# Layers 0 and 1 of a four-layer convolution kernel: ScalarE's input statistics by a table of their own, and the turn-back one slot later

## The reference

```
# layer 0: the normalised image, shifted down and right by offsets from its own channel means, zero outside
offsets = clip(mean(gn(x), (H, W)) @ W + b, 0, 28).astype(int32)
x = x + where(inside, gn(x)[i - dy, j - dx], 0)
# layer 1: a 3x3 convolution of the signs with the sum of four sign matrices
x = x + conv3x3(sign(gn(x)), sum_m sign(W[m])) + b.sum(0)
# layers 2 and 3: 32 x 32 modes (DCT along columns, real FFT along rows) mixed by R, and a 1x1 convolution
x = x + relu(inverse(R . modes(gn(x))) + gn(x) @ W.T + b)
```

## Time and profile before

| what | us |
|---|---|
| median of 3 runs | 3662.61 (3637.99 to 3672.19) |
| the profiled execution | 3671.81 |
| its span, first to last instruction | 3670.1 |
| mean granted TensorE clock over the span | 0.887 |
| busy in the span: PE, DVE, ACT, POOL | 2996.9, 2730.0, 1511.0, 553.5 |

### The profile page before, as it was taken

How to read it: one execution, slowest core, us unless ns; L and a number is a source line. 1 busy time by engine, 2 the same in 40 slices (tenths; PEclk the granted TensorE clock), 3 DMA queues, 4 the chain that set the end, 5 groups by cost and what they waited for, 6 DMA issues and landing times. The chain is left out here.

```text
span 3670.1 us, 59833 instructions
## 1 busy us (share of the span) xinstructions
PE 2996.9 (82%) x17264; PEld 1392.2 (38%) x17264; DVE 2730.0 (74%) x3908; ACT 1511.0 (41%) x2728; POOL 553.5 (15%) x1059
## 2 busy tenths in 40 slices
PE   0189988888998889889937898888888737999997
PEld 0034443443444334444435333333333316444443
DVE  3888878887888888787233867777776642999998
ACT  3476766766676676674443222222222232000000
POOL 2333323332332333221010000000000010000000
PEclk9988878888888888889867999999999857999998
DMA  5577656666666676664176465655546255999998
GB/s 149 171 221 224 202 183 205 215 202 188 214 198 190 203 219 205 193 199 154 74 147 243 194 260 200 243 220 227 237 201 252 101 121 193 337 373 390 389 378 298
DMA packets 255824, 808.76 MB, mean 220 GB/s; under 512 B 85466, under 2 KB 119774, under 8 KB 244724
## 3 DMA queue, kind: packets, MB, share of 16 engines
q1 hardware_dynamic: 163796, 370.64, 30.8%
q10 hardware_dynamic: 58368, 316.72, 22.2%
q0 software_dynamic: 33376, 118.13, 11.3%
HBM read 479.39 MB, written 329.56 MB: 220 GB/s over the span
## 5 line engine op out<-in xcount | busy, mean ns | idle before, releaser
L975 POOL DMA_DIRECT2D A_rin<-in_x x1008 | 507.5, 504 | 1158.2 <-DVE A_image L818 527.7
L1488 ACT ACTIVATE B_junk<-B_im,B_nk 128x896 bf16<-128x896 f32 x224 | 232.8, 1039 | 717.7 <-DVE B_im L1546 582.9
L476 PE MATMUL A_cps<-A_sign,A_cfull 128*128 128x448 bf16 x1344 | 415.0, 393 | 10.2 <-issue 10.2
L1739 PE MATMUL C_ring<-C_im,C_wnorm 128*128 128x448 f32 x896 | 387.9, 571 | 25.8 <-DVE C_ubuf L1796 20.4
L852 DVE SCALAR_TENSOR_TENSOR A_image<-A_cps,A_cbias,A_image 128x896 f32<-128x896 f32 x224 | 256.9, 1147 | 195.5 <-PE A_cps L476 192.2
L504 PE MATMUL A_aps<-a_k_ident,A_image 128*112 128x128 f32 x1792 | 290.1, 305 | 131.1 <-DVE A_image L852 72.8
L1434 PE MATMUL B_ring<-B_im,B_wnorm 128*128 128x448 f32 x896 | 384.9, 571 | 7.2 <-DVE B_wnorm L1517 5.0
L622 ACT ACTIVATE A_tout<-A_aps 112x512 f32<-112x512 f32 x448 | 249.6, 591 | 333.7 <-PE A_aps L504 214.5
L1406 PE MATMUL B_ring<-B_rout,b_k_rowf 128*64 128x512 f32 x896 | 279.3, 707 | 118.4 <-DVE B_rout L1539 118.4
L481 PE MATMUL A_cps<-A_sign,A_cedge 32*32 32x448 bf16 x1344 | 374.0, 388 | 0.0
L483 PE MATMUL A_cps<-A_sign,A_cedge 32*32 32x448 bf16 x1344 | 373.8, 387 | 0.0
(11 more groups left out here) (198 smaller groups left out, 3697.4 us busy)
## 6 DMA issues: line engine op xcount, KB each, us to landing
A_rin<-in_x POOLq DMA_DIRECT2D x1008, 112.0 KB, 3.7
A_rin<-in_x SPq DMA_DIRECT2D x1008, 112.0 KB, 3.6
x2s<-A_image ACTq DMA_DIRECT2D x112, 896.0 KB, 4.6
B_im<-x2s SPq DMA_DIRECT2D x112, 896.0 KB, 10.2
x3s<-B_im ACTq DMA_DIRECT2D x112, 896.0 KB
C_im<-x3s SPq DMA_DIRECT2D x112, 896.0 KB, 12.9
out<-C_rout ACTq DMA_DIRECT2D x192, 256.0 KB
out<-C_rout ACTq DMA_DIRECT2D x192, 192.0 KB
```

The costliest lines, as they stand in the source:

```text
L476: return nc.tensor.matmul(banks[:, s, 0:LPN], cfull[:, tap, :], lines(n, s, slice(0, P), 0, tap), start=(tap == 0), stop=(tap == 2), skip_ ...
L975: pool.dma_start(rin[slot][32 * i:32 * i + 32, :], rows[:, first * C:(first + CHQ) * C]).then_inc(in_lower[slot], 16)
L1739: nc.tensor.matmul(slot(add_place(e))[:, lane % 2, 0:2 * SIZE], wnorm[par][:], im[par][:, EVN * e:EVN * (e + 1)].rearrange("p (m s) -> p s ...
```

## The change

ScalarE's tiles of input statistics get a table of their own, STAT_BY, one or two in each of slots 1 to 11. X_BY and S_BY are moved: a third input tile in slot 0, the first shifted tile in slot 1. The turn-back of unit n stands in slot n + 2, behind convolution n + 2; with it copy_back, forward_cols (slots 4, 6 to 14, and 15), copy_rows and the ring's numbers. Statistics 0 of VectorE moves from slot 11 to 12, statistics 1 behind the shifted tiles of slot 12, and TensorE's statistics 4 from slot 13 to 14.

```
--- before.py
+++ after.py
@@ -250,8 +250,9 @@
         x_pix = x.rearrange("b r q c -> (b r q) c")
         pad_pix = xpad.rearrange("r q c -> (r q) c")
 
-        X_BY = [2, 4, 6, 7, 8, 10, 11, 12, 14, 16, 16, 16, 16, 16, 16, 16]
-        S_BY = [1, 2, 3, 4, 5, 6, 7, 8, 9, 10, 12, 14, 16, 16, 16, 16]
+        X_BY = [3, 4, 6, 7, 8, 10, 11, 13, 14, 15, 16, 16, 16, 16, 16, 16]
+        S_BY = [0, 1, 2, 3, 4, 5, 6, 7, 8, 10, 12, 14, 16, 16, 16, 16]
+        STAT_BY = [0, 1, 3, 4, 6, 7, 8, 10, 11, 13, 14, 16, 16, 16, 16, 16]
 
         def x_tiles(s):
 
@@ -280,7 +281,7 @@
 
         def stat_tiles(s):
 
-            return x_tiles(s - 1) if s else range(0)
+            return range(STAT_BY[s - 1] if s else 0, STAT_BY[s])
 
         def junk_place(has_v, has_x):
 
@@ -318,7 +319,7 @@
 
             if isinstance(b, int) and b == 0:
                 return 2 * n + half
-            return ((2, 5, 8, 12, 15, 18)[n] if n < 6 else 8 + 2 * n) + half
+            return ((3, 6, 10, 13)[n] if n < 4 else 8 + 2 * n) + half
 
         def spec_step(s):
 
@@ -326,7 +327,7 @@
 
         def ring_t(k):
 
-            return (0, 1, 4, 7, 10, 11, 14, 17)[k]
+            return (0, 1, 2, 5, 8, 9, 12, 15)[k]
 
         def average_no(b, i):
 
@@ -555,22 +556,20 @@
                         conv(b, s)
                     if has_tail and s < 8:
                         spectrum(b - 1, spec_step(s), ring_base(b))
-                    if has_v and s in (3, 5, 7, 9, 11):
-                        forward_cols(b, q, (s - 3) // 2)
-                    if has_v and 1 <= s <= UNITS:
-                        turn_back(b, q, s - 1)
+                    if has_v and s in (4, 6, 8, 10, 12, 14):
+                        forward_cols(b, q, (s - 4) // 2)
+                    if has_v and s >= 2:
+                        turn_back(b, q, s - 2)
                     if has_tail and s == 3:
                         spectrum(b - 1, 4, ring_base(b))
                     if has_x and s in (12, 13):
                         statistics(b + 1, s - 11)
-                    if has_v and s == 13:
-                        forward_cols(b, q, 5)
-                    if has_s and s == 13:
+                    if has_s and s == 14:
                         statistics(b, 4)
+                    if has_x and s == 15:
+                        statistics(b + 1, 3)
                     if has_v and s == 15:
                         forward_cols(b, q, 6)
-                    if has_x and s == 15:
-                        statistics(b + 1, 3)
 
             body(-1, 2, False, True, True, False)
             body(0, 0, True, True, True, False)
@@ -676,8 +675,8 @@
                         copy_rows(b - 1, NSPEC - 1)
                     if has_tail and s < 7:
                         copy_cols(b - 1, spec_step(s), ring_base(b) + ring_t(spec_step(s)))
-                    if has_v and 1 <= s <= UNITS:
-                        copy_back(b, q, s - 1)
+                    if has_v and s >= 2:
+                        copy_back(b, q, s - 2)
                     if has_v and s == 6:
                         copy_rows(b, 0)
                     if has_tail and s == 3:
@@ -692,8 +691,8 @@
                         square(b, q, s - 1)
                     if has_x and s == 14:
                         lower(b + 1, (q + 2) % 3)
-                    if has_v and s in (9, 13):
-                        copy_rows(b, (s - 5) // 4)
+                    if has_v and s in (10, 14):
+                        copy_rows(b, (s - 6) // 4)
                     for k in stat_tiles(s) if has_x else ():
                         x_tile(b + 2, (q + 2) % 3, k, tile_no(b, x_at(k)))
 
@@ -909,8 +908,8 @@
                         add_conv(b, q, s)
                     if has_tail and s == 10:
                         image_statistics(b - 1, far)
-                    if has_x and s in (11, 12):
-                        statistics(b + 1, s - 11, far)
+                    if has_x and s == 12:
+                        statistics(b + 1, 0, far)
                     for k in x_tiles(s) if has_x else ():
                         if k == 0 and has_tail:
                             dve.wait_ge(stored[far], 16 * GROUPS * (third + 1))
@@ -927,6 +926,8 @@
                         signs(q, 2 if s < 5 else 3, (s % 3,) if s < 5 else (s - 6,))
                     for k in s_tiles(s) if has_s else ():
                         add_shifted(b, nxt, k, s_at(k, has_x))
+                    if has_x and s == 12:
+                        statistics(b + 1, 1, far)
                     if has_s and s == 12:
                         center(b)
                     if has_s and s == 13:
```

9 lines of the change are left out of this document (5 added, 4 removed).

## The result

The changed kernel takes 3808.8 us (median of 4 runs, 3789.7 to 3813.7) against 3663.5 of the kernel before: a ratio of 1.039, 95% interval 1.034 to 1.044. That is 145 us slower where 100 were forecast (3763, range 3690 to 3825). The direction and the range held, and so did most of the places. The sum was a third too small, and the experiments show that one of its reasons was wrong.

What follows compares the result with a forecast made beforehand. TensorE was taken to end last from convolution 0 to about 8, then VectorE to the image's end; 4.5 + 0.8 + 1.5 + 0.6 + 0 = 7.4 us an image, times 13.5 = 100 us, giving 3763 us (range 3690 to 3825).

Steps and rivals of the forecast that it cites:

- The wait in front of centered: End of an image: VectorE waits at centered for TensorE's statistics 4, 4.5 us an image, taken between 2.2 and 7.0.
- The idle time itself: TensorE at statistics 1, held by VectorE's later statistics 0: idle up to 5.5 us an image, coming out cold.
- Much slower: Rival: TensorE cold through the turn of the image, centered wait 7.0, 12.2 us an image, 3822 us; chance 0.16.
- The start of the next image: Copy_back 13 behind lower delays forward_cols 6 and convolution 0 by 4.6 us; net 0.8 to add 8 (-1.0 to +1.6).
- What pays it back: By convolution 8 TensorE has one turn-back and one forward_cols less behind it, giving back 3.8 us an image.
- VectorE's extra work behind add 8: End of an image: one shifted tile more and one input tile less on VectorE, 1.5 us (+1.0 to +2.0).
- the 0.6: End of an image: statistics 4's matmul, which ended 0.6 us before centered, now ends right at it, +0.6 us.
- The idle time in front of shifted tiles: Image's front: a third input tile in slot 0 saves at most 37.4 us of load waits over the stage; taken as 0.
- The levelled statistics: ScalarE's regrouped tiles: late copies move from slots 2 and 4 to 3 and 5, two for two, 0 us (-4 to +2).
- the rule: ScalarE's copy is late where a two-tile slot precedes one with a copy and no forward_cols ahead of the turn-back; 1.6 us late.
- Faster: the clock stays up: Rival: copies come in time, gaps and low clock go, net 5 us an image saved, 3598 us; chance 0.12.

Runs made afterwards that it cites:

- e_order: Changed kernel with TensorE's statistics 1 moved behind convolution 13 and turn-back 11, and forward_cols 5 and turn-back 12 ahead of statistics 2: 3753.3 us (1.021).
- e_mean4: Changed kernel with TensorE's statistics 4 directly behind statistics 2, ahead of forward_cols 5 and turn-back 12, and ScalarE's root ahead of copy_back 12: 3821.6 us (1.045).
- e_order_rows: e_order with ScalarE's copy_rows 2 and copy_back 13 also put ahead of root and lower: 3697.2 us (1.011).
- e_parity: Changed kernel with ScalarE's two-tile slots moved from 2 and 4 to 3 and 5, nothing else: 3663.5 us (1.003).
- e_level_odd: e_level with ScalarE's two-tile slots at 3 and 5 in place of 2 and 4: 3761.3 us (1.028).
- e_level: Changed kernel with the turn-back and all that goes with it as before, leaving the levelled statistics alone: 3594.0 us (0.976).
- e_parity_order: e_order_rows with ScalarE's two-tile slots at 3 and 5: 3535.5 us (0.971).
- e_lag: Changed kernel with X_BY, S_BY, ScalarE's statistics tiles and VectorE's statistics 0 and 1 as before, leaving the turn-back's one-slot lag alone: 3680.4 us (1.002).

## Why the prediction was right, and where it was wrong

**The wait in front of centered** (4.5 forecast) was measured at 4.6 to 4.8 us an image, 4.0 to 4.3 in ten images and 6.0 to 6.5 in four: right in place and size, and in its cause, TensorE's idle time at statistics 1 and the chain behind it, in which convolution 13 runs at the lower clock. The idle time itself was mis-sized, 9.4 us where the working had up to 5.5, and was over 5 us in every image. That is the sign that the rival "Much slower" asked for, and still its 7.0 did not come, since the clock was up again by forward_cols 5 in most images. That 4.5 came out so near is in part luck: it was a middle taken between 2.2 and 7.0. As a price, e_order takes the wait away and gains 3.4 us an image by the period (116.6 to 113.1), 4.1 by the medians and 4.8 by the ratios (each over 13.5 images); e_mean4, which takes it away with the same work still between centered and forward_cols 6, gains nothing.

**The start of the next image** (0.8 forecast) is the term that failed. The times were right: forward_cols 6 at 8.3 us, convolution 0 at 11.9. Wrong was the step "What pays it back: by convolution 8 TensorE now has one turn-back and one fc less behind it". It took convolutions 0 to 8 for one path on TensorE. But VectorE waited 5.0 us for convolutions 0 and 1 and then not at all for 2 and 3: there VectorE is the last again, so what it lost at 0 and 1 is lost before any payback. The trace of the kernel before has this too, no wait for a convolution in units 0 to 2 and 0.1 us in unit 3; the prediction read TensorE as last from convolution 0 on. With both waits behind lower out (e_order to e_order_rows) the term measures 5.6 us by the periods, 4.1 by the medians and 2.8 by the ratios; the profiled execution of e_order was its slowest and that of e_order_rows its fastest, so 5.6 is its top. All three are above the 1.6 that the prediction had as the worst. And two things behind lower held forward_cols 6, not one; I read only the copy_back.

**VectorE's extra work behind add 8** (1.5) and the 0.6 were not tested by themselves. The idle time in front of shifted tiles fell by some 3 us an image, which I had put at 0. By size the two would about cancel; no run shows it.

**The levelled statistics** (0, "two for two") was right as a sum and hid the largest effect in the case. The copy waits are 55.9 and 60.2 us, as forecast, and the rule was the right one: late behind a two-tile slot unless a forward_cols stands ahead of the turn-back. What I did not do was to ask each half alone. Levelling moves the late copies to slots 3 and 5, where the old forward_cols hides them: 70 us faster. The lag moves forward_cols to 4 and 6 and uncovers them again. Nor did I price them in full: the prediction gave one of them and its low clock 4 us, and two of them cost 10 us an image or more, by three pairs of runs (periods: e_parity against the changed kernel 10.5, e_level_odd against e_level 10.1, e_parity_order against e_order_rows 10.9; the medians and ratios give 10 to 14). The price depends on the place: e_lag has 41.3 us of these waits, in slots 2 and 3, and loses nothing. Why was not tried.

The steps from the changed kernel to e_parity_order, in periods: 116.6, less 3.4 for the chain, 5.6 for the start and 10.9 for the late copies, is 96.6. They are successive differences, so they add up by construction, and each holds in this order only: with the two turns still in, the late copies are worth 10.5. The kernel before, at 106.2, had the late copies and neither of the others.

**The rivals.** "Faster: the clock stays up" was given 0.12 and asked for exactly the right sign, a slot 3 without a wait for A_colpart. It is what e_level is: 70 us faster, 65 forecast. In the whole change the late copies undid it; with them out the turn's losses still stand against it, and e_parity is no faster than the kernel before. "Much slower" (3822) was the nearest number to the result, for partly the right reason: the centered wait was 4.6, not 7.0, but the start cost more than its 1.6. The Trainium skill ("TensorE: Matmul & The Clock Gate", section "What's actually happening") states that TensorE's clock is throttled by default and that activity releases it. By that rule alone the prediction had the centered wait at 7.0; the trace has 6.0 to 6.5 in four images and 4.0 to 4.3 in ten, in which forward_cols 5 already ran at the upper clock (1.91 at 1191.54).

## What to carry to other kernels

When two edits move work by slots, write down for each slot what hides what, for each edit alone and for both. Here a forward_cols ahead of a turn-back hid a late copy or did not, and a sum over the whole change (two late copies before, two after) came to nothing. Price a gap on TensorE with the stretch at the lower clock behind it, not by its length alone. And before taking away a wait, ask what the engine will stand at next: one edit here only uncovered a second wait, one left the same work ahead of the next image, and neither gained, while putting independent work ahead of the waiting instruction gained at once.

## What was not expected of the hardware

Behind a gap of 2.1 us the granted clock can fall. In the changed kernel each of twelve images has two such gaps; the clock fell within 2 us of the end of the first in all twelve, for 13.7 us in eleven of them, and at the second in only four. TensorE's timeline at such a late copy, and the busy time of the 10 us that follow (us, PE, PEld, DVE, ACT, POOL, clock, DMA, GB/s):

```profile
1230.65 0.70 PE L505 MATMUL A_aps<-a_k_ident,A_image 128*112 128x128 f32 x4 [2.13 <-ACT A_colpart L639]
```
```profile
1234.00:1244.00 10.00, 10.00 (x37) 3.45 (x36) 6.25 (x9) 3.78 (x7) 2.30 (x6) 0.50 0.35 102
```

TensorE is busy all of the 10 us, at the lower level (1.2 GHz), and it was busy on both sides of the gap. Added up from the granted clock over twelve images, the changed kernel spends 16.8 us an image at that level between adds 3 and 7, e_parity 0.0: 3.7 us of copy gaps taken away (4.5 to 0.8) took away 16.8 us of low clock. That stretch is 0.0 in all four kernels without a late copy (e_parity, e_level and the two with the order changed as well), 12.0 in the kernel before, 11.5 in e_level_odd and 5.6 in e_lag.

The kernel before shows how much of the price is the clock and how much the gap. Its image of 98.5 us (from 598.93 to 697.38) has both gaps in full, and no low clock behind them:

```profile
612.62 0.70 PE L504 MATMUL A_aps<-a_k_ident,A_image 128*112 128x128 f32 x4 [1.94 <-ACT A_colpart L640]
629.27 0.70 PE L504 MATMUL A_aps<-a_k_ident,A_image 128*112 128x128 f32 x4 [2.02 <-ACT A_colpart L640]
```
```profile
612.00:640.00 28.00, 25.22 (x166) 12.46 (x167) 22.54 (x33) 23.38 (x44) 10.49 (x20) 1.00 0.75 229
```

Another image has the same (gaps that end at 1254.23 and 1270.84, no low clock behind them) and takes 97.5 us; the other ten, at 104.3 to 112.2, have 12 to 18 us of low clock between adds 3 and 7. So most of the price of a late copy seems to be the low clock behind it, and not the gap itself. That rests on two images of twelve; no run changes the clock and leaves the gaps. The whole stage of the two kernels, 300 to 1500 us, first the changed kernel, then e_parity_order:

```profile
300.00:1500.00 1200.00, 978.28 (x5386) 439.39 (x5384) 883.21 (x1615) 729.73 (x1390) 335.09 (x654) 0.81 0.59 183
```
```profile
300.00:1500.00 1200.00, 1092.94 (x6562) 505.02 (x6560) 1073.99 (x1972) 897.01 (x1711) 411.32 (x800) 0.90 0.73 224
```

In the same 1200 us VectorE has 883 us of work in the one and 1074 in the other; TensorE does 22% more matmuls (6562 for 5386) in 12% more busy time. What decides whether a gap is followed by a low stretch was not tried; gaps of the same length have both.
